# Context codes made on GpSimd during attention, and a first output projection that takes both column halves of a head in turn in eight PSUM banks

## What is computed

```python
x = x + attn(layernorm(x), ctx, ctx, wq, wk, wv, wo)   # 32 query heads, 8 key/value heads of 128, rotary, softmax
x = x + router_ffn(layernorm(x))                       # softmax over 64 experts, top 8, bias mix
x = x + fake_quant(layernorm(x), s1, z1) @ fake_quant(ctx, s2, z2)
x = x + ffn(layernorm(x), nf4(w1), nf4(w2), nf4(w3))   # silu gate, weights through NF4 codes, hidden size 2752

def fake_quant(x, s, z):
    q = clip(round(x / s + z), 0, 255)
    return (q - z) * s
```

## Time and profile before

| what | value |
|---|---|
| median of 3 runs | 3098.54 us |
| profiled execution | 3100.92 us |
| its span (first to last instruction) | 3099.1 us |
| attention stage, about | 781 to 1738 us |
| projection slots 0 to 63 (batch 0) | 1745.3 to 1955.2 us |
| projection slots 64 to 127 (batch 1) | 1955.2 to 2211.7 us |
| TensorE busy over the span | 2934.0 us (95%) |
| VectorE, ScalarE, GpSimd busy | 2283.1, 1929.3, 1126.7 us |

### The profile page before, as it was taken

One profiled execution on the slowest core, in us unless ns is written; L12 is line 12 of the kernel. 1 busy time (PEld: TensorE's weight loads), 2 busy tenths in 40 slices (PEclk: granted clock), 3 DMA queues, 4 the chain that ended last, 5 costly groups with the idle time before them and its releaser, 6 DMA issues. The chain is left out here.

```text
span 3099.1 us, 39391 instructions
## 1 busy us (share of the span) xinstructions
PE 2934.0 (95%) x14134; PEld 2396.3 (77%) x14144; DVE 2283.1 (74%) x3330; ACT 1929.3 (62%) x2627; POOL 1126.7 (36%) x670
## 2 busy tenths in 40 slices
PE   7999999998999999999999889989999999999999
PEld 6878788886888888888888667766876777777787
DVE  5878778786888888888888454787466678887733
ACT  4665666665888888888888587544333456555511
POOL 5728268887233333333332455443100221111100
PEclk9999999999999999999999999999999999999999
DMA  5455434444222222222221577543644562222211
GB/s 180 142 175 165 141 125 142 146 136 151 91 79 79 90 89 79 79 96 79 79 94 61 180 271 270 200 132 136 237 177 170 176 223 84 82 82 82 69 34 58
DMA packets 231489, 399.89 MB, mean 129 GB/s; under 512 B 19840, under 2 KB 106880, under 8 KB 229248
## 3 DMA queue, kind: packets, MB, share of 16 engines
q1 hardware_dynamic: 225792, 372.22, 35.8%
q0 software_dynamic: 5504, 25.17, 2.4%
HBM read 279.48 MB, written 117.83 MB: 128 GB/s over the span
## 5 line engine op out<-in xcount | busy, mean ns | idle before, releaser
L1120 DVE CUSTOM_DVE_ANT_0 at_sc<-at_s,at_mk 128x1024 f32<-128x1024 f32 x256 | 312.1, 1219 | 108.7 <-issue 107.2
L1135 DVE TENSOR_TENSOR at_ptl<-at_t,at_pth 128x512 fp32r<-128x512 f32 x512 | 326.8, 680 | 32.0 <-ACT at_pth L1082 31.7
L1082 ACT ACTIVATE at_pth<-at_t 128x512 fp32r<-128x512 f32 x512 | 276.8, 594 | 99.6 <-PE at_t L1182 99.3
L1072 ACT ACTIVATE at_pr<-at_sc,at_low 128x1024 f32<-128x1024 f32 x256 | 295.5, 1154 | 64.3 <-DVE at_low L1120 35.3
L134 PE MATMUL fr_acc<-fr_xh,fr_wh 128*128 128x512 f32 x768 | 300.2, 391 | 7.7 <-POOL fr_wl L726 5.9
L136 PE MATMUL fr_acc<-fr_xh,fr_wl 128*128 128x512 f32 x768 | 299.3, 390 | 0.0
L135 PE MATMUL fr_acc<-fr_xl,fr_wh 128*128 128x512 f32 x768 | 299.3, 390 | 0.0
L1182 PE MATMUL at_t<-ident,at_pr 128*128 128x128 f32 x2048 | 269.3, 274 | 24.1 <-DVE at_ptl L1135 23.8
L1182 PEld LDWEIGHTS at_t<-ident,at_pr 128*128 128x128 f32 x2048 | 235.3, 140 | 70.0 <-issue 36.3
L243 ACT ACTIVATE fr_nf_above<-fr_nf_raw,sharp 128x1024 f32<-128x1024 f32 (+1 forms) x196 | 215.8, 1102 | 113.6 <-DVE fr_nf_val L269 52.7
L134 PE MATMUL tl_pa<-tl_ring_h 128*128 128x512 f32 x512 | 212.2, 414 | 41.0 <-POOL tl_ring_l L1999 22.9
(11 more groups left out here) (229 smaller groups left out, 7879.5 us busy)
## 6 DMA issues: line engine op xcount, KB each, us to landing
tl_ring<-o_d SPq DMA_DIRECT2D x128, 256.0 KB, 3.8
tl_ring<-in_L_xattn_wo SPq DMA_DIRECT2D x128, 256.0 KB, 4.5
tl_raw<-dq SPq DMA_DIRECT2D x63, 512.0 KB, 3.7
fr_raw<-in_L_xattn_wq SPq DMA_DIRECT2D x32, 512.0 KB, 4.7
q_d<-fr_res SPq DMA_DIRECT2D x64, 256.0 KB, 2.4
rows<-q_d SPq DMA_DIRECT2D x64, 256.0 KB, 2.7
at_inv_row<-r_d SPq DMA_DIRECT2D x64, 256.0 KB, 3.5
o_d<-at_ot SPq DMA_DIRECT2D x64, 256.0 KB, 2.0
```

Of the source, the lines that this page charges most:

```text
L1072: act.activation(pr[:, n % 2], sc[:, n % 2], ACT.Exp, bias=low[:, n % 2:n % 2 + 1], scale=-1.0, accum_out=sums[:, h % 2, quarter:quarter + ...
L1082: act.activation(pt[0][:, h % 2, j * HALF:(j + 1) * HALF, (n % QT) * P:(n % QT + 1) * P], t_ps[:, j], ACT.Copy).then_inc(t_hi.sem, 1)
L1120: dve.tensor_tensor_reduce(sc[:, n % 2], s_ps[:, n % 2], mk[:, bb * QT + n % QT], -1.0, -NEG, ALU.add, ALU.min, low[:, n % 2:n % 2 + 1]).t ...
L1135: dve.tensor_tensor(pt[1][sl], t_ps[:, j], f32(pt[0][sl]), ALU.subtract).then_inc(t_lo.sem, 1)
```

## The change

1. **Codes in attention.** The 16 context tiles are made in the attention stage by GpSimd alone, with three instructions each (`tensor_scalar` with two operations): scale at step 15 + 12c, round and clip from above at the next step, clip from below and code at step 19 + 12c. The scale comes from two broadcast loads and one reciprocal on VectorE. SyncE loads tile c at step 5 + 12c and stores it at step 22 + 12c. ScalarE's three instructions, GpSimd's clip, and the context loads and stores leave the tail stage; its load of codes (L1605 onward) waits for nothing more.
2. **Both halves in turn.** Slots 0 to 63 handle head q // 2 and column half q % 2. Odd slots load only wo's half and make high and low halves of 512 columns instead of 1024; they use the head's output of the even slot before. High halves of an odd slot's successor in the ring wait one head longer. Sweep 0 adds up in `pa`, sweep 1 in `pc` and `pt`; sweep 2 starts in `pa` after the adds of sweep 0, which come at slot 63; those of sweep 1 come at slot 64.
3. **What had to move.** Router weights go from slots 50 and 51 to 65 and 66, column sums from 56 and 57 to 67 and 68. The first four NF4 units of the tail have both ramps in SBUF; from unit 4 on the second is `pt` again. `xT` and `qaT` get buffers of their own.

```diff
--- attention_stage
+        CX_FROM, CX_EVERY, NC = 15, 12, B * KT
+        def context_at(n):
+            c, r = divmod(n - CX_FROM, CX_EVERY)
+            return [c] if r == 0 and 0 <= c < NC else []
@@ SyncE
+            def load_context(c):
+                if c >= 2:
+                    sp.wait_ge(cx_coded, c - 1)
+                sp.dma_start(cx[:, c % 2], context[c // KT, c % KT * P:(c % KT + 1) * P, :]).then_inc(cx_in[c % 2], 16)
+            def store_context(c):
+                sp.wait_ge(cx_coded, c + 1)
+                sp.dma_start(qb_d[c], cx_code[:]).then_inc(cx_out, 16)
             def do_step(n):
                 for kind, x in fetches(n):
                     fetch(kind, x)
+                for c in context_at(n + 10):
+                    load_context(c)
+                for c in context_at(n - 7):
+                    store_context(c)
@@ GpSimd
+            def scale_context(c):
+                if c == 0:
+                    pool.wait_ge(cx_ready, 1)
+                pool.wait_ge(cx_in[c % 2], 16 * (c // 2 + 1))
+                pool.tensor_scalar(cx[:, c % 2], cx[:, c % 2], cx_par[:, 2:3], cx_par[:, 1:2], ALU.mult, ALU.add).then_inc(cx_scaled, 1)
+            def round_context(c):
+                pool.wait_ge(cx_scaled, c + 1)
+                pool.tensor_scalar(cx[:, c % 2], cx[:, c % 2], ROUND, ROUND + QMAX, ALU.add, ALU.min).then_inc(cx_rounded, 1)
+            def code_context(c):
+                pool.wait_ge(cx_rounded, c + 1)
+                if c:
+                    pool.wait_ge(cx_out, 16 * c)
+                pool.tensor_scalar(cx_code[:], cx[:, c % 2], ROUND, ROUND + QMID, ALU.max, ALU.subtract).then_inc(cx_coded, 1)
             def do_step(n):
                 if (n - COPY_LAG) % QT == 0 and exists(n - COPY_LAG):
                     scale_out((n - COPY_LAG) // QT)
+                for c in context_at(n):
+                    scale_context(c)
+                for c in context_at(n - 1):
+                    round_context(c)
+                for c in context_at(n - 4):
+                    code_context(c)
                 for kind, x in fetches(n):
--- Plan
+    def head(self, q):
+        return (q % 2, q // 2) if self.double(q) else divmod(q, HQ)
+    def double(self, q):
+        return 0 <= q < 2 * HQ
+    def whole(self, q):
+        return not self.double(q) or q % 2 == 0
     def swept(self, q):
-        return [q // HQ - 1] if 0 < q <= self.FIRST and q % HQ == 0 else []
+        return {2 * HQ - 1: [0], 2 * HQ: [1], 3 * HQ: [2], 4 * HQ: [3]}.get(q, [])
--- tail_stage
-        chain = Chain(plan.BASE, (plan.BASE[0] - 8, plan.BASE[1] - 16), plan.BASE[0] - 14)
+        chain = Chain(plan.BASE, (plan.BASE[0] + 3, plan.BASE[1] - 16), plan.BASE[0] + 1)
+        MOVED = 4
+        nf1.moved = (MOVED, [above[:, 0], pt[:].rearrange("p s n -> p (s n)")])
+        def sweep_bank(w, t):
+            return pa[:, t] if w != 1 else (pc if t < 2 else pt)[:, t % 2]
+        def ring_free(q):
+            return q - RING + (2 if plan.double(q - RING) and plan.whole(q - RING) else 1)
@@ SyncE, load_head
+                if plan.whole(q):
+                    sp.dma_start(ring[:, q % 4, 0], o_d[h][:, b * SQ:(b + 1) * SQ]).then_inc(ring_in[q % 4], 16)
@@ ScalarE, high
                 if q >= RING:
-                    act.wait_ge(heads, q - RING + 1)
-                act.activation(ring_h[:, q % RING], ring[:, q % 4], ACT.Copy).then_inc(ring_hi, 1)
+                    act.wait_ge(heads, ring_free(q))
+                act.activation(ring_h[:, q % RING, ring_parts(q)], ring[:, q % 4, ring_parts(q)], ACT.Copy).then_inc(ring_hi, 1)
@@ ScalarE, loop
+                    if (u, j) == (MOVED, 0):
+                        act.wait_ge(o_added, 2 * QT)
@@ TensorE, project
-                q = w * HQ + h
+                q = 2 * h + w if w < 2 else w * HQ + h
                 r = q % RING
+                ro = r if plan.whole(q) else (q - 1) % RING
                 for t in range(QT):
-                    if h == 0 and w:
-                        pe.wait_ge(o_added, (w - 1) * QT + t + 1)
+                    if h == 0 and w >= 2:
+                        pe.wait_ge(o_added, (0 if w == 2 else 2) * QT + t + 1)
@@ TensorE, link
-                if k >= 2:
+                if k < 2:
+                    pe.wait_ge(o_added, 2 * QT)
+                else:
```

More of the change, by code:

```diff
@@ L168, in __init__, with ramps_of @@
         self.finished = event("nf_finished", 2)
+    def ramps_of(self, n):
+        return self.moved[1] if self.moved and n >= self.moved[0] else self.ramps
     def blocks(self, ap, width):
@@ L1220, in __init__ @@
     def __init__(self):
-        self.slots = [("head", q // HQ, q % HQ) for q in range(self.FIRST)]
+        self.slots = [("head", *self.head(q)) for q in range(self.FIRST)]
         self.turn_no, self.turn_slot, self.turns = {}, {}, {}
@@ L1441, in tail_stage @@
             colsum = sb_first("colsum", [P, D], F32)
-            rows = sb_first("rows", [P, 2, D], F32)
-            codes = sb_first("codes", [P, 2, D], BF16)
-            above = (sb_first("above", [P, D], F32)[:], pt[:].rearrange("p s n -> p (s n)"))
+            xT = sb_first("xT", [P, DC, P], F32)
+            qaT = sb_first("qaT", [P, 2, DC, P], BF16)
+            above = sb_first("above", [P, 2, D], F32)
             nf1_buffers = [sb_first(f"nf{k}", [P, 2, D], F32) for k in range(2)] + [above, am1]
@@ L1536, in tail_stage, with ring_landed, ring_parts @@
         RING, LEAD = plan.RING, plan.RING - 2
-        NC = B * KT
-        CONTEXT_FROM = 5
-        def context_slot(n):
-            return CONTEXT_FROM + 3 * n
+        def ring_landed(q):
+            return 16 * sum(2 if plan.whole(k) else 1 for k in range(q % 4, q + 1, 4))
+        def ring_parts(q):
+            return slice(0 if plan.whole(q) else 1, 2)
+        def sweep_bank(w, t):
+            return pa[:, t] if w != 1 else (pc if t < 2 else pt)[:, t % 2]
+        def ring_free(q):
+            return q - RING + (2 if plan.double(q - RING) and plan.whole(q - RING) else 1)
         def x_slot(t):
@@ L1584, in load_head @@
             def load_head(q):
-                w, h = divmod(q, HQ)
+                w, h = plan.head(q)
                 b, n = divmod(w, 2)
@@ L1998, in low @@
                 pool.wait_ge(ring_hi, q + 1)
-                pool.tensor_tensor(ring_l[:, q % RING], ring[:, q % 4], f32(ring_h[:, q % RING]), ALU.subtract).then_inc(ring_lo_p, 1)
-            def clip_context(n):
-                pool.wait_ge(ctx_rounded, n + 1)
-                pool.tensor_scalar(rows[:, n % 2], rows[:, n % 2], ROUND + QMAX, ROUND, ALU.min, ALU.max).then_inc(ctx_clipped, 1)
+                pool.tensor_tensor(ring_l[:, q % RING, ring_parts(q)], ring[:, q % 4, ring_parts(q)],
+                                   f32(ring_h[:, q % RING, ring_parts(q)]), ALU.subtract).then_inc(ring_lo_p, 1)
             def pad(i, xx, q):
@@ L2044, in _ @@
                     fetch(i, j)
-                for n in range(NC):
-                    if q == context_slot(n) + 2:
-                        clip_context(n)
                 for kind, b, t, h in chain.due("pool", q):
```

87 lines of the change are left out of this document (26 added, 61 removed).

## The result

The changed kernel took 3069.81 us (median of 4 runs, 3067.53 to 3074.71) against 3098.02 us beside it: 28.2 us less by the medians. The ratio, estimated from all eight runs, is 0.9914, 95% interval 0.9902 to 0.9925, which is 26.6 us less (23.2 to 30.4). The forecast was 3070 us, from a sum of -28.2. That the medians hit it to a tenth is chance: the four runs of each kernel spread over 5 to 7 us.

What follows compares the result with a forecast made beforehand. The crowded slots 0 to 63 were taken to be bound by the late feed of weights, not by TensorE. Terms -33.3 + 2 + 1.6 + 1.5 = -28.2 us, set on the median of 3098.5, gave 3070 us, range 3060 to 3084.

Steps and rivals of the forecast that it cites:

- Pace and start: Slots 0 to 63: full pace of 2.715 us a slot plus 2.8 us of start, 176.6 us, a gain of 33.3 us.
- what the ring gives back: Slots 0 to 63: odd slots' later high halves cost nothing; NF4 unit ends cost 2 us, between 0 and 14.
- the sign named in advance: Slots 0 to 63: ScalarE's high halves would wait for TensorE's matmuls instead of for loads.
- The mechanism of the loss: Slots 0 to 63: ScalarE waits for GpSimd, SyncE for ScalarE (70.9 us), ScalarE for SyncE's loads: a loop of order.
- The adds and the moved work: Around slots 63 to 70: a 6.2 us wait goes; moved work fills a 6.53 us wait, delaying transposes 1.6 us.
- GpSimd in attention: Attention: 48 new GpSimd instructions at 1.5 us, 72 us in all, which nobody but SyncE waits for.
- rival D: Attention: each GpSimd instruction stretches a VectorE one by 0.89 us, all 43 us reach TensorE; +13, 3111 us; chance 0.04.
- The price of contention: Attention: GpSimd stretches VectorE instructions with two SBUF inputs by up to 6 us; 1.5 us reaches the total, ends 0 and 43.
- The rule: Attention: elementwise codes belong on VectorE, about twice as fast; the prediction declined, counting 58 us on an engine busy 803 of 957.
- A: Slots 0 to 63: ring depth and NF4 waits bind, three unit ends cost 4.6 us more each; -16, 3082 us; chance 0.13.
- B: After slot 64: VectorE's chain comes later by more than two instructions, 6 us; -24, 3075 us; chance 0.10.
- C: Whole kernel: attention costs nothing, the start loads less, the second half starts less behind; -36, 3062 us; chance 0.09.

## Why the prediction was right, and where its steps failed

*Pace and start.* 176.6 us were predicted for slots 0 to 63, and 2 for what the ring gives back: 178.6. Measured 178.4. Two slots of 4.86 and 3.36 us at the start are 2.8 over the pace, and slots 51, 62 and 63 are 0.5 us or so over each. That the feed was the bound holds; so does the longer wait of odd slots at no cost: ScalarE waited 40.0 us for TensorE to free the ring. Of the sign named in advance that is one half only: its waits for loads were to give way, and they stayed at 31.6 us.

*The mechanism of the loss failed in part.* "This is a loop of order" put SyncE's wait of 70.9 us at its centre. Taken away alone it gave 1.9 us. Nor were the wo loads late because of it: ScalarE's wait for them, 30.3 us before, is 27.7 with that wait gone and 31.6 in the changed kernel. What starved the ring was in the main ScalarE's queue: context instructions and the wait for the clip, both ahead of the high halves (by the prices above, which are partly extrapolated). The sum was not touched, since the change removes both, but the reason was half wrong: I took the longest wait in the list for a cause.

*The adds and the moved work.* The 6.2 us wait after sweep 0 is gone. For the moved work the number was right by luck and the mechanism wrong. The prediction let VectorE's two column instructions delay the normalised x, and TensorE wait 1 to 3 us for it before the first transposes. There was no such wait: VectorE had done the normalising by 1950.4 us, and TensorE came to the transposes only at 1951.7. The moved work took the whole of the old wait of 6.53 us and 1.8 us more, which happens to be near the 1.6 predicted. A part of that was a wait of a kind not foreseen: the first column sums stood 2.0 us, as the row above has it, for ScalarE to copy the router weights out of the same two banks, behind a fold that waited 9.05 us for VectorE. Slots 64 to 127 took 0.7 us more in all.

*GpSimd in attention.* The term mis-sized most is its work: 1.5 us an instruction predicted, 2.96 measured (142 / 48), outside the bound of 2.41 that I drew from its slowest form. It cost nothing because the cover was counted right: nobody but SyncE waits for the codes, and even 128 us more moved the ratio by no more than 0.0004, 1 us. The sign named for rival D, instructions above 2.4 us, thus came true without D. The price of contention, 1.5 us predicted, is some 2 us by the length of the scores, and the stretching of VectorE behind it 2.9 us where up to 6 were allowed.

*The rule.* The Trainium skill (GPSIMD Engine Reference, Performance versus the Vector engine) calls GpSimd wrong for ordinary elementwise work, VectorE being about twice as fast. On the instructions its direction is right and its factor too small, 142 against 44 us; on the kernel it would have cost 13 us, because VectorE was the scarcer engine. The contention of the same page of the Trainium skill (Specifications) did show, and small: VectorE's instructions with two inputs in SBUF rose by 2.9 us in all, and by 8.3 with GpSimd's load doubled.

*The rivals.* A: no stall at the ends of units, although SyncE's NF4 wait nearly doubled. It does come with more steps: 191.7 us at one in every slot. B: the transposes came 1.8 us later, not 6, and VectorE's chain was not what they waited for. C: its 36 us lie outside the interval of 23.2 to 30.4. D is excluded: 96 GpSimd instructions in attention lengthened the scores by 3 to 6 us against none.

*The sum.* -33.3 + 2 + 1.6 + 1.5 = -28.2 predicted. Measured by stretch, in one execution of each, -31.5 for slots 0 to 63 (the prediction: -31.3), +0.7 for 64 to 127 (+1.6), +0.2 before them (+1.5), and +4.3 in the feed-forward, most likely scatter, -26.3 together. The ratio says -26.6 (23.2 to 30.4 less, from its interval and 3098), the medians -28.2.

## What to carry to other kernels

Price a wait by taking it away alone before calling it the cause: the longest one, on SyncE, was worth 2 us of 71, a shorter one in the queue that feeds the bound some 7 of 15. Put side work on the engine whose queue nobody waits for, even if it is three times slower there. Once a crowded stretch runs at its pace, look at what it leaves idle: here two units of other work moved out of the feed-forward cost that stretch 13 us and saved the feed-forward 27 to 32, and with the steps spread anew the whole gained more than half as much again as by the change itself (3070 to 3052 us). And when a predicted sum comes out, look at each term: one of these was right for a reason that did not happen.

## What was not expected of the hardware

GpSimd's `tensor_scalar` on 128x1024 fp32 differs by the pair of operations and not by their number. Multiply-add with constants takes 1.06 us, with scalars from a tile 1.33; min-max 1.04. Add-min and max-subtract take 3.64 us, add-subtract 3.88, and a single add 2.78, more than a multiply-add. All six ran in the same kernel on the same two buffers, on different values. VectorE needs 0.76 us for the add-min that costs GpSimd 3.8. Why some pairs are fast, and whether the values matter, was not tried.
